# First half of the adjacency in two transfers, and the loads of x in another order

## The reference

```python
def _L0_gnn_ref(x, adj, W, b):
    agg = jnp.matmul(adj, x)
    out = jnp.matmul(agg, W.T) + b
    return jax.nn.relu(out)
h = jnp.maximum(_layernorm(x, axis=-1), 0.0)
x = x + _L0_gnn_ref(h, adj, L0_gnn_W, L0_gnn_b)
```

## Time and profile before

| what | value |
|---|---|
| median of 3 executions | 380.52 us (380.36 to 380.57) |
| profiled execution, its own time | 380.32 us |
| its span, first to last instruction | 378.5 us |
| TensorE matmuls | 375.0 us busy, 99% of the span |
| VectorE, ScalarE, GpSimd | 56%, 48%, 13% of the span |
| HBM traffic | 211 GB/s over the span |

### The profile page before, as it was taken

One profiled execution on the slowest core, in us unless ns is written; L12 is line 12 of the kernel. 1 busy time (PEld: TensorE's weight loads), 2 busy tenths in 40 slices (PEclk: granted clock), 3 DMA queues, 4 the chain that ended last, 5 costly groups with the idle time before them and its releaser, 6 DMA issues.

```text
span 378.5 us, 4516 instructions
## 1 busy us (share of the span) xinstructions
PE 375.0 (99%) x1650; PEld 308.4 (81%) x1650; DVE 212.8 (56%) x295; ACT 180.8 (48%) x227; POOL 47.3 (13%) x88
## 2 busy tenths in 40 slices
PE   9999999999999999999999999999999999999997
PEld 5888888888888888888888888888888888888885
DVE  5999988886444444565564535444464444444424
ACT  4878776765343434543643343434355243434341
POOL 4576732321000000001001000000000100000000
PEclk9999999999999999999999999999999999999999
DMA  7999887658655665556866856565656775656203
GB/s 265 345 314 301 253 300 243 206 193 299 202 192 198 177 210 185 203 175 213 290 207 208 293 178 207 177 208 182 203 187 193 258 240 197 185 204 184 95 2 111
DMA packets 22774, 80.25 MB, mean 212 GB/s; under 512 B 2496, under 2 KB 2880, under 8 KB 22752
## 3 DMA queue, kind: packets, MB, share of 16 engines
q1 hardware_dynamic: 19584, 68.30, 54.5%
q0 software_dynamic: 3168, 11.67, 8.9%
HBM read 75.76 MB, written 4.19 MB: 211 GB/s over the span
## 4 chain that ended last, share of the span: by engine, by line
PE 99%; DVE 0%; issue 0%
PE bank L443 92%; PE bank L486 6%; PE bank L499 1%; DVE out_sb L340 0%
## 5 line engine op out<-in xcount | busy, mean ns | idle before, releaser
L443 PE MATMUL bank<-adj_hi,h_sb 128*128 128x512 f32 x1024 | 254.7, 389 | 0.0
L246 DVE TENSOR_TENSOR adj_lo<-adj_in,adj_hi 128x1024 fp32r<-128x1024 f32 x126 | 154.5, 1226 | 144.2 <-ACT adj_hi L361 144.2
L443 PEld LDWEIGHTS bank<-adj_hi,h_sb 128*128 128x128 f32 x1024 | 192.3, 188 | 40.0 <-ACT h_sb L371 0.3
L361 ACT ACTIVATE adj_hi<-adj_in 128x1024 fp32r<-128x1024 f32 x126 | 133.5, 1060 | 175.9 <-PE bank L443 172.9
L443 PE MATMUL bank<-adj_lo,h_sb 128*128 128x512 f32 x512 | 137.8, 389 | 0.0
L443 PEld LDWEIGHTS bank<-adj_lo,h_sb 128*128 128x128 f32 x512 | 96.1, 188 | 20.0
L238 POOL DMA_DIRECT2D out_t_dram<-out_sb x3 | 2.2, 726 | 205.5 <-DVE out_sb L340 205.5
L220 POOL TENSOR_TENSOR rstd<-var_eps,minus_half 128x1 f32<-128x1 f32 x32 | 27.3, 853 | 4.5 <-DVE var_eps L271 1.9
L371 ACT ACTIVATE h_sb<-centred,rstd 128x256 fp32r<-128x256 f32 x32 | 15.9, 497 | 3.4 <-POOL rstd L220 3.1
L381 ACT ACTIVATE centred<-x_sb,neg_mean 128x256 f32<-128x256 f32 x31 | 15.5, 499 | 3.1 <-DVE neg_mean L286 2.2
L292 DVE SCALAR_TENSOR_TENSOR h_sb<-centred,rstd,h_sb 128x256 fp32r<-128x256 f32 x32 | 15.3, 477 | 0.0
(11 more groups left out here) (26 smaller groups left out, 42.8 us busy)
## 6 DMA issues: line engine op xcount, KB each, us to landing
adj_in<-adj_t_dram SPq DMA_DIRECT2D x126, 512.0 KB, 4.1
xt_sb<-x_t_dram POOLq DMA_DIRECT2D x4, 1024.0 KB, 7.6
x_sb<-x_dram POOLq DMA_DIRECT2D x7, 512.0 KB, 7.1
out_t_dram<-out_sb POOLq DMA_DIRECT2D x3, 1024.0 KB, 4.9
adj_in<-adj_t_dram SPq DMA_DIRECT2D x4, 256.0 KB, 4.5
out_t_dram<-out_sb SPq DMA_DIRECT2D x3, 256.0 KB, 2.0
x_sb<-x_dram POOLq DMA_DIRECT2D x3, 128.0 KB, 6.0
w_sb<-w_t_dram POOLq DMA_DIRECT2D x1, 256.0 KB, 6.6
```

What stands on the lines that cost most here:

```text
L246: nc.vector.tensor_tensor(adj_lo[:, k, :], adj_in[:, k, :], adj_hi[:, k, :].bitcast(fp32), ALU.subtract).then_inc(s_lo, 1)
L361: nc.scalar.activation(adj_hi[:, k, :], adj_in[:, k, :], ACT.Copy).then_inc(s_hi, 1)
L443: last = nc.tensor.matmul(bank(g, kb, c)[:], h_sb[:, t, hp, kb * P:(kb + 1) * P], adj_parts[ap][:, n % U, chunk(c)], start=(t == 0 and (hp ...
```

## The change

Three things are changed. The first chunk of adjacency (512 columns of tile 0, group 0) is loaded by two transfers of 256 columns with a semaphore each; DVE rounds each as it lands, and TensorE takes the high by high pass of this chunk as four matmuls of 256 columns in place of two of 512. The filler matmuls behind the first landing are one of 128 columns in place of two of 256. And x of tile 1 is issued by SP behind the first three chunks (that is, behind four transfers of adjacency) in place of by POOL at the start, while the 512 KB of x for tiles 4 to 7 are issued by POOL behind the root of tile 1 in place of the root of tile 0.

```diff
-    WARM_ON = 2
+    WARM_ON = 1
...
             load_x(sp, 0)
-            load_chunk(0, 0)
+            g, t = UNITS[0]
+            for i, cols in enumerate(QUARTERS):
+                at = g * GW + cols.start
+                sp.dma_start(adj_in[:, 0, cols], adj_v[:, t, at:at + HALF]).then_inc(s_q[i], 16)
             load_chunk(0, 1)
             load_chunk(1, 0)
+            load_x(sp, 1)
             load_chunk(1, 1)
...
         def _(pool):
-            load_x(pool, 1)
...
                 root(t)
                 if t == 0:
-                    for i in range(2, U + 1):
-                        load_x(pool, i)
+                    load_x(pool, 2)
+                    load_x(pool, 3)
+                if t == 1:
+                    load_x(pool, U)
...
             def first_rounded():
 
-                dve.wait_ge(s_early[0][0], 16)
-                nc.vector.tensor_copy(adj_hi[:, 0, chunk(0)], adj_in[:, 0, chunk(0)]).then_inc(s_hi, 1)
+                for i, (cols, made) in enumerate(zip(QUARTERS, (s_quarter, s_hi))):
+                    dve.wait_ge(s_q[i], 16)
+                    nc.vector.tensor_copy(adj_hi[:, 0, cols], adj_in[:, 0, cols]).then_inc(made, 1)
...
+            def first_sums(cols):
+
+                for kb in range(KB):
+                    nc.tensor.matmul(bank(0, kb, 0)[:, cols], h_sb[:, 0, 0, kb * P:(kb + 1) * P],
+                                     adj_hi[:, 0, cols], start=(cols.start == 0), stop=False,
+                                     skip_group_check=True)
+
             def early_unit(n):
 
                 pe.wait_ge(s_hhi, 1)
-                pe.wait_ge(s_hi, made_chunk(n, 0))
-                add_up(n, [0], 0, 0)
+                if n == 0:
+                    pe.wait_ge(s_quarter, 1)
+                    first_sums(QUARTERS[0])
+                    pe.wait_ge(s_hi, 1)
+                    first_sums(QUARTERS[1])
+                else:
+                    pe.wait_ge(s_hi, made_chunk(n, 0))
+                    add_up(n, [0], 0, 0)
...
-            pe.wait_ge(s_early[0][0], 16)
-            warm_up(WARM_ON, BANK // 2)
+            pe.wait_ge(s_q[0], 16)
+            warm_up(WARM_ON, BANK // 4)
```

More of the change, by code:

```diff
@@ L31, in bass_preln_gnn_residual @@
     BANK = 512
+    HALF = BANK // 2
+    QUARTERS = (slice(0, HALF), slice(HALF, BANK))
     CHUNKS = 2
@@ L98, in bass_preln_gnn_residual @@
         s_adj = [sem(f"adj_landed{k}") for k in range(U)]
+        s_q = [sem(f"adj0_quarter{i}_landed") for i in range(2)]
         s_early = [[sem(f"adj{t}_chunk{c}_landed") for c in range(CHUNKS)] for t in range(EARLY)]
@@ L111, in bass_preln_gnn_residual @@
         s_hlo = sem("h_lo_made")
+        s_quarter = sem("first_adj_quarter_made")
         s_hi = sem("adj_hi_made")
```

## The result

The changed kernel takes 381.27 us (median of 16 executions, 380.59 to 382.53); the kernel before takes 380.54 (16 beside it, 380.36 to 380.79). The ratio is 1.0020, interval 1.0014 to 1.0027: slower by 0.7 us. Its executions spread over 1.94 us against 0.43; in the larger sets of 22 to 35 executions beside the experiments the kernel before spreads over 0.7 to 1.0. I had forecast 380.4 and a range up to 380.9. The profiled execution of the changed kernel took 380.76, so it is among the shorter of the sixteen; it shows 0.44 us of the 0.73.

A forecast was written before the change was run, and what follows sets the result against it. TensorE, busy 99% of the span, bounds the kernel, and DVE's chain decides the start: 0.13 off the profiled 380.32 gives 380.19, plus 0.20 for the median 380.39, say 380.4 us. Range 380.05 to 380.9.

The forecast's parts named there:

- The start: TensorE's first real matmul at 5.18, 0.31 earlier; low pass of the first chunk at 6.45 instead of 6.58, gain 0.13.
- The casts: DVE's rounding of 256 columns takes 0.33, ending near 4.45 and 4.78, ahead of the high part of h at 5.09.
- the rival without support here: DVE's casts stand behind POOL's root of tile 0: gain 0.08 instead of 0.13, 380.44 us; chance 0.06.
- the hold: DVE's first cast, ready at 4.12, stands until POOL's root ends at 4.55; low part of h at 5.18 at most.
- The later transfers: DMA engines full from 5 us, so bytes ahead count: x of tile 1 lands at 7.0, units issued 0.8 later, nothing lost.
- My first rival: Latency stays with the issue: second quarter lands at 5.3, x of tile 1 at 7.85; +0.3, 380.8 us; chance 0.14.
- The wait behind the landing: ACT's rounding of unit 2 and h of tile 1 behind it: no term in the prediction, no cost counted.
- the bracket at TensorE behind 6.5: Sign of being wrong: a wait of TensorE behind 6.5 us, where matmuls were forecast at 0.227 without gaps.
- x of tiles 4 to 7: 512 KB issued at 9.3 instead of 5.6, landing at 15.3 to 16.8; nothing lost until the landing passes 17.8.
- the fillers: TensorE ahead of the first real matmul: 384 columns fewer, which ran while it waited anyway; gain nothing.
- 0.43 apart behind 6 us: Sign of being wrong: TensorE's matmuls at the 1.2 GHz spacing behind 6 us.
- my fourth rival: TensorE's clock rises later because fillers are fewer: 1.6 us more at 1.2 GHz, slower by 0.8, 381.3 us; chance 0.04.

The follow-up runs named there:

- h_ahead: Changed kernel with ACT making the high part of h of tile 1 ahead of the rounding of unit 2; 381.13 us, ratio 1.0023.
- two_small: Kernel before with two more transfers of 1 KB on SP between the fourth chunk and unit 2; 380.43 us, ratio 1.0002.
- small_early: Kernel before with two more transfers of 1 KB on SP behind the first chunk; 381.57 us, ratio 1.0028.
- fill_old: Changed kernel with two fillers of 256 columns behind the first landing again instead of one of 128; 381.17 us, ratio 1.0013.
- x4_early: Changed kernel with x of tiles 4 to 7 issued behind the root of tile 0 again; 381.24 us, ratio 1.0023.
- halves_only: Changed kernel with x loaded in the order and on the queues of before; 380.80 us, ratio 1.0014.
- x1_act_late: Changed kernel with x of tile 1 issued by ACT, placed behind its first activation in the code, instead of by SP; 380.91 us, ratio 1.0008.
- x_order_only: Kernel before with the changed kernel's order of x and no halves; 380.64 us, ratio 1.0007.
- halves_h: Changed kernel with x loaded as before and the high part of h of tile 1 ahead of unit 2's rounding on ACT; 380.97 us, ratio 1.0014.
- rows_split: Kernel before with the first chunk in two transfers of 64 rows, one cast behind both; 381.34 us, ratio 1.0031.
- q2_on_act: Changed kernel with the second quarter issued by ACT and x loaded as before; 380.92 us, ratio 1.0018.
- act_both: Changed kernel with the second quarter and x of tile 1 issued by ACT instead of SP; 381.03 us, ratio 1.0022.

## Why the prediction was wrong

**The start: right, a little too good.** The quarters landed at 3.93 and 4.76 (I took 3.9 and 4.4), and the second cast was done at 5.07, just ahead of the high part of h. The high part of h was next to be late, weight load at 5.14 and low part of h at 5.13 came as forecast. The matmul of the low pass came at 6.52 instead of 6.45. The term that was off is the first matmul's: the second stood 0.38 behind it, though 256 columns at 1.2 GHz take 0.21. A weight load that no matmul ahead of it covers is a likely reason, but it was not tested, and in h_ahead the second stood only 0.24 behind. The low part of the chunk was done at 6.21 as forecast, so not DVE's chain but TensorE's own pace set 6.52: four pieces until 6.06, two matmuls of 0.23 after it.

**The casts: right, and the rival without support here.** A cast took 0.29 (I took 0.33). It ran from 4.05 while POOL's root ran from 3.97 to 4.55, and neither is stretched against 4.78's cast and the root before (0.59). So the exclusion that the Trainium skill states (SBUF — State Buffer, "Who interferes with whom") does not show here for this pair; a cast is among the operations that it names, in a mode with two ports, and no run shows the mode of this one. In the prediction I also read only one order of the pair, a root that starts ahead of DVE's subtraction (0.55). Where the subtraction starts first, the root is stretched, in the same trace and in each of the eleven cases that it holds; it ends 0.40 to 0.42 behind the subtraction:

```profile
12.42 1.24 DVE L246 TENSOR_TENSOR adj_lo<-adj_in,adj_hi 128x1024 fp32r<-128x1024 f32 x1
12.66 1.40 POOL L220 TENSOR_TENSOR rstd<-var_eps,minus_half 128x1 f32<-128x1 f32 x1
```

So DVE does hold up POOL in these rows, and that POOL holds up DVE is what they do not show. The 0.05 that the prediction charged for the hold was too much even by its own terms: casts done at 5.21, with the overlap of 0.08 that it used elsewhere, let the low part of h start at 5.13.

**The later transfers: the step that failed.** I wrote that the engines are full from 5 us on, "so what counts is the bytes ahead of a transfer". That put x of tile 1 at 7.0 (it landed at 3.06 + 3.7 = 6.8) and looked right, but I never asked the same of the next transfer in the queue, unit 2. I took the share of the kernel before (1.05) as given, though the change alters what fills it. It fell to 0.74 at 4 to 5 us, and unit 2 landed at 9.88 instead of 8.89. A smaller slip stands in the same paragraph: two issues more at 0.44 to 0.47 are 0.9, not 0.8, and 0.95 was measured. My first rival said that latency stays with the issue: for unit 2 it did, 5.86 against 5.82. That is a coincidence. The same late issue behind full transfers has 4.7 (two_small), behind thin ones 6.5 (small_early), and in h_ahead, fill_old and x4_early, with the changed kernel's own transfers ahead of it, 6.2, 6.5 and 5.5. The rival's own price rested on x of tile 1 and the second quarter, and both came in time.

**The wait behind the landing: put at nothing.** The prediction gave ACT's queue no line for unit 2. What stands behind its rounding is h of tile 1, and TensorE needs that for the unit's first matmul. In every execution with the old order on ACT that ran into this wait, the first matmul of unit 2 stands 1.53 behind the landing: 9.88 and 11.41 here, 9.89 and 11.42 (halves_only), 10.09 and 11.62 (x1_act_late), 10.18 and 11.71 (x_order_only), 10.48 and 12.01 (small_early), 10.52 and 12.05 (fill_old). That is 1.06 for the rounding, 0.49 for h, less a little overlap. Before the change the unit was due at 11.11, so a landing up to 9.58 was free, 0.7 behind the 8.89 of before. The changed kernel passes this edge, and every tenth beyond it is paid. This is the bracket at TensorE behind 6.5 that the prediction named as a sign of being wrong. The order on ACT is a link of the chain and not a cause by itself: with h ahead of the rounding the edge is 9.63, and neither h_ahead nor halves_h gained.

**The spread: explained in part.** Past the edge, the landing's own variation reaches the end of the kernel. Four profiled executions with the changed kernel's transfers ahead of unit 2 (x4_early, the changed kernel, h_ahead, fill_old) have it at 9.48, 9.88, 10.24 and 10.52 and took 380.47, 380.76, 381.11 and 381.45. With the old order on ACT the edge gives the time: 380.32, and the landing beyond 9.58, and the 0.11 of the second matmul make 380.73 for the changed kernel (measured 380.76), 380.74 for halves_only (380.82), 380.94 for x1_act_late (380.99), 381.03 for x_order_only (381.07), 381.33 for small_early (381.40) and 381.37 for fill_old (381.45). The kernel before has 0.7 of slack there. That the longest one (382.53) is made the same way is not shown; it was not profiled.

**x of tiles 4 to 7, the fillers, the clock.** All three at no cost, as forecast: x4_early and fill_old are where the changed kernel is. Its x of tiles 4 to 7 landed at 9.02 + 5.86 = 14.9, ahead of the 16.7 at which it was wanted. No matmuls stood 0.43 apart behind 6 us. So the 381.3 of my fourth rival (a later rise of the clock) agrees with the median by accident.

**Which part of the change did it.** The halves alone cost 0.4, the order of x alone 0.2 (not clear of the noise), casts and filler nothing. Both add a thin slot to the front of SP's queue; small_early adds two with nothing else and costs 1.15. Open is what happens within the DMA engines: whether they run short, or are held up (in rows_split and small_early they count as busy while moving little). No experiment here separates these.

## What to carry to other kernels

Before splitting an early transfer to start sooner, read what the issuing queue has to supply in the first microseconds: a transfer of 1 KB took the same 0.47 us on the queue as one of 512 KB, and where such slots stood among the first transfers, what followed landed later; behind four full transfers they cost nothing. Follow each later landing to the engine that waits for it and then to what stands behind that wait on the same engine; here 0.7 us of slack lay there, and the change used 1.0 in the profiled execution. The first real matmul came 0.35 us sooner, and of that 0.04 was left before unit 2, since the next operands came no sooner. Take more than one landing before building on it: the same load varied by 0.8 to 1.0 us between executions.

## What the runs showed of the hardware

- Two slots of 1 KB among the first transfers of SP raise the latency of a 512 KB load issued at 4.0 us from 4.7 to 6.5 us; the same two slots behind four transfers of 256 KB raise nothing (one profiled execution each; 381.57 against 380.43 us in the median).
- The issues on SP of transfers with 128 rows start 0.42 to 0.50 us apart, mostly 0.47, whether they carry 1, 128, 256 or 512 KB (one of 0.59 in q2_on_act); in rows_split, the two transfers of 64 rows and the chunk behind them took 0.60 to 0.63 each, for a reason that no run shows.
- The landing of the same load behind the same transfers differs between executions: 8.58 to 9.39 us in three, 9.48 to 10.52 us in four.
- A root on GpSimd (one column) that starts while VectorE subtracts two tiles ends 0.40 to 0.42 us behind the subtraction (eleven cases in the kernel before, 1.25 to 1.48 us long, against 0.55 for one that starts first); the subtraction keeps its 1.24.
- A transfer on ACT's queue issued at the same 0.74 us as SP's first delays the latter's landing from 2.2 to 3.1 us behind its issue (q2_on_act; 3.0 in act_both), with 128 KB each; issued 0.06 later, at 0.80, it is 2.5 (x1_act_late).
- A DMA issue placed behind a table load and an activation in ACT's code went out at 0.80 us, ahead of their end (2.2 us), as nothing in the code made it wait (x1_act_late).
- TensorE's change from 1.2 to 2.4 GHz, read from the spacing of the fillers and the first matmuls, is not fixed to the start of the kernel: between 5.7 and 5.9 us in the changed kernel's profile, and ahead of the tenth filler in x_order_only's (0.22 apart from 4.10 on). The waits that follow swallow it: fill_old, where it came near 4.1 us too, has the longest profiled execution of this order of loads (381.45).
